# Graph attention kernel on one core: VectorE takes the next group's logits and the turned one-hots behind the fifth message instead of behind the second

## What is computed

```python
z = (x @ W).reshape(N, num_heads, head_dim)
el = jnp.sum(z * attn_l, axis=-1)
er = jnp.sum(z * attn_r, axis=-1)
e = jax.nn.leaky_relu(el[src] + er[dst], NEG_SLOPE)
m = jax.ops.segment_max(e, dst, num_segments=N)
ex = jnp.exp(e - m[dst])
denom = jax.ops.segment_sum(ex, dst, num_segments=N)
alpha = ex / denom[dst]
msg = alpha[:, :, None] * z[src]
out = jax.ops.segment_sum(msg, dst, num_segments=N)
```

## Time and profile before

| what | us |
|---|---|
| median of 3 runs (3047.36 to 3049.39) | 3047.59 |
| the profiled execution, its own time | 3049.01 |
| its span, first to last instruction | 3047.3 |
| first to last gather issue, first layer | 247.5 to 873.8 |
| the same, second layer | 1095.5 to 1721.7 |
| the same, third layer | 1937.5 to 2563.3 |

### The profile page before, as it was taken

The page is one execution under the profiler, slowest core; times in us unless marked ns, Lnnn a source line. Parts: engine busy times, 40 slices in busy tenths (PEclk is TensorE's granted clock), DMA queues, the critical chain, the costliest instruction groups (busy, mean ns, idle before and its releaser), DMA issues.

```text
span 3047.3 us, 57262 instructions
## 1 busy us (share of the span) xinstructions
PE 2681.5 (88%) x14059; PEld 1839.2 (60%) x14060; DVE 2055.3 (67%) x3890; ACT 1244.9 (41%) x2607; POOL 1495.0 (49%) x1528
## 2 busy tenths in 40 slices
PE   3997999998989979999899899788899888659998
PEld 2884555555558855555555588555555555447776
DVE  6776888888887768888878877455555555663332
ACT  1224555555554445555555544222323223521111
POOL 1005666666632156666666411466666664114443
PEclk9998999999999979999999999799999999979999
DMA  6448988989968889999989678888888998967776
GB/s 211 167 146 269 304 306 303 304 306 302 305 203 213 212 247 305 303 307 304 306 299 306 231 199 221 237 295 297 294 300 298 294 297 270 406 211 146 145 146 119
DMA packets 218702, 787.26 MB, mean 258 GB/s; under 512 B 44050, under 2 KB 75938, under 8 KB 217983
## 3 DMA queue, kind: packets, MB, share of 16 engines
q0 software_dynamic: 127632, 604.14, 63.8%
q1 hardware_dynamic: 73230, 133.39, 14.3%
q10 hardware_dynamic: 17760, 48.79, 4.0%
HBM read 665.13 MB, written 133.50 MB: 262 GB/s over the span
## 4 chain that ended last, share of the span: by engine, by line
PE 53%; DVE 22%; issue 13%; ACT 3%; another core or an unknown queue 3%; DMA 2%; SPq 2%; POOL 1%; DVEq 1%; ACTq 1%; POOLq 0%
PE PS L1026 29%; DVE arena L1466 6%; PE PS L957 5%; PE PS L1153 5%; PE PS L1142 4%; PE PS L959 3%; DVE parts L1483 3%; PE PS L1001 2%; DVE W L1466 2%; DMA arena<-table,src_k 2%; SPq L479 1%; DVE arena L1341 1%; DVE arena L1330 1%; DVE arena L1331 1%
## 5 line engine op out<-in xcount | busy, mean ns | idle before, releaser
L652 POOL DMA_INDIRECT arena<-table,src_k x945 | 946.9, 1002 | 488.6 <-issue 225.2
L1026 PE MATMUL PS<-arena,S 128*128 128x384 f32 (+1 forms) x1848 | 694.7, 509 | 58.6 <-issue 49.5
L1466 DVE TENSOR_TENSOR arena<-arena,PS 128x768 f32<-128x768 f32 x630 | 575.0, 945 | 0.9 <-issue 0.5
L1026 PEld LDWEIGHTS PS<-arena,S 128*128 128x128 f32 x1848 | 333.0, 192 | 275.3 <-issue 142.3
L1026 PE MATMUL PS<-parts,S 128*128 128x384 f32 (+2 forms) x1332 | 338.6, 374 | 54.2 <-issue 41.3
L652 POOL DMA_INDIRECT W<-table,src_k x300 | 297.8, 993 | 155.4 <-issue 68.9
L1026 PE MATMUL PS<-arena,S_weighted 128*128 128x384 f32 (+1 forms) x840 | 318.7, 515 | 35.3 <-issue 32.9
L1001 PEld LDWEIGHTS PS<-erp,ST_b 128*128 128x128 bf16 x3735 | 194.8, 97 | 240.6 <-issue 173.1
L598 POOL DMA_DIRECT2D table<-arena x75 | 41.7, 555 | 560.1 <-DVEq L1353 384.2
L809 ACT ACTIVATE apart<-iota_row,dst_k 128x128 f32<-128x128 f32 x830 | 261.5, 389 | 58.4 <-issue 34.4
L1026 PEld LDWEIGHTS PS<-parts,S 128*128 128x128 f32 x1332 | 223.5, 192 | 99.8 <-issue 90.2
(11 more groups left out here) (286 smaller groups left out, 4275.1 us busy)
## 6 DMA issues: line engine op xcount, KB each, us to landing
local_b<-local SPq DMA_DIRECT2D x249, 160.0 KB
mixed<-sums ACTq DMA_DIRECT2D x75, 384.0 KB
arena<-mixed SPq DMA_DIRECT2D x75, 384.0 KB, 4.3
table<-arena POOLq DMA_DIRECT2D x50, 396.0 KB, 3.6
arena<-table SPq DMA_DIRECT2D x50, 384.0 KB, 4.8
arena<-table,src_k POOLq DMA_INDIRECT x945
table<-arena POOLq DMA_DIRECT2D x25, 384.5 KB, 4.8
out<-last_bias POOLq DMA_DIRECT2D x25, 384.0 KB, 6.3
```

The lines of the kernel that those rows point to most:

```text
L652: nc.gpsimd.indirect_dma_start(edge_row(l, k % U)[:, 0:table_width(l)], None, table[l][:, :], bass.IndirectOffsetOnAxis(src_k[:, k:k + 1]. ...
L1026: o = nc.tensor.matmul(flat[:, bass.ds(odd * 1024 + 512 * c, n)], onehot, row[:, c * HALF:c * HALF + n], start=False, stop=True, skip_grou ...
L1466: nc.vector.tensor_tensor(z, z, a, ALU.mult).then_inc(s_msg, 1)
```

## The change

In `weigh` the calls of `turned` and of the steps leave the loop over the five messages and come behind it, the steps first and `turned` after them. Before, `turned` came behind message 1 (the second), the first step directly after it, the second step behind message 2 and, with one head, the third and fourth behind message 3.

```diff
@@ -1496,12 +1496,11 @@
                         message(g, i, jj, j)
                         if H > 1 and j >= 2 and jj * G + j - 2 in SPLIT[l]:
                             rest(g, i, jj, j - 2)
-                        if j == 1 and turn_next:
-                            turned(g + NBUF, i + 1, jj)
-                        if steps and 1 <= j <= min(3, len(steps)):
-                            steps[j - 1]()
-                        if j == 3 and steps and H == 1:
-                            steps[3]()
+                    if steps:
+                        for step in steps:
+                            step()
+                    if turn_next:
+                        turned(g + NBUF, i + 1, jj)
```

## The result

| | median, us | runs |
|---|---|---|
| before | 3048.36 | 7 (3045.02 to 3051.80) |
| changed | 3059.40 | 7 (3053.31 to 3063.23) |

The ratio is 1.003, 95% interval 1.0018 to 1.0041: the change makes the kernel slower by 0.3%. The forecast was 3045.0 us and no measurable change. The profiled execution of the changed kernel took 3053.31 us (span 3051.6), the quickest of its seven, so its trace explains 4.3 us of span, and not the other 6 or 7.

A forecast was written before the change was run, and what follows sets the result against it. Gathers in flight, about five landing every 7.5 us, were taken as the bound. Inside the sweeps 0 us, ends -0.5 - 0.5 - 1.5 = -2.5 us, from the median 3047.6 to a forecast of 3045.0 us, range 3037 to 3062.

The forecast's parts named there:

- the released messages: Inside the sweeps, three messages per group no longer held behind the gather wait; costed at nothing, slots being free 5 us early.
- the collision of `turned` with POOL: Rival: `turned` near a landing collides with POOL's gather issue, 0.7 us per group, 174 us if nothing hid it; chance 0.02.
- The price of one stall: DVE's wait for `rest` at a block's close: 2.2 us, or 3.9 us in the group of slots 10 to 14.
- 63 us a layer: DVE's stalls for `rest` at a layer's 24 closes inside the sweep, 18 x 2.2 + 6 x 3.9, 45 us more than before.
- it fits, with 42 us left: First layer: 66 us added in total against DVE's 108 us of spare time, so the sweep gets no longer.
- The chain's term: Logits, exponentials, then first message now precede every group's messages: 0.25 us more per group, 21 us over a layer's 83 groups.
- 25 to 50 us: The wait in front of the logits, line 1449, expected to remain in the changed profile.
- -0.5 us for each of the first two layers: Ends of the first two layers' edge sweeps: the middle taken between 2.8 us earlier and 1.9 us later.
- The gain of 2.8 from the held messages: End of a sweep: where DVE waits for the last landing, its end comes 2.8 us earlier.
- The third layer's -1.5: End of the third layer's sweep: a gain of 0 to 2.8 us, taken as 1.5, because PE is behind there.
- VectorE and ScalarE become the bound: Rival: stalls of `rest` behind closes in the first two layers use up DVE's spare time, 3062 to 3077 us; chance 0.28.
- All ends gain in full: Rival: each layer ends 2.8 to 4 us earlier, 8 to 12 us in all, giving 3037 to 3039 us; chance 0.25.

The follow-up runs named there:

- e2: Kernel before with only `turned` moved behind the fifth message, the steps left as before; quick gathers: 2812.49 us, ratio 0.9997 to the kernel before.
- e10: The changed kernel as it stands, run with quick gathers: 2966.93 us, ratio 1.0569 to the kernel before.
- e12: Kernel before with the new order in the last three groups of each layer alone; quick gathers: 2807.65 us, ratio 0.9996 to the kernel before.
- e15: Changed kernel with ACT's one-hots moved ahead of the exponentials; quick gathers: 2850.72 us, ratio 1.0148 to the kernel before.
- e16: Kernel before with only ACT's one-hots moved ahead of the exponentials; quick gathers: 2851.03 us, ratio 1.0158 to the unedited kernel before.
- e6: The changed kernel again, in another job with slow gathers: 3085.34 us, ratio 1.0028 to the kernel before.
- e7: Kernel before with, for 12 heads only, logits behind the fourth message, `higher` then `turned` behind the fifth; slow gathers: 3077.95 us, ratio 1.0006 to the kernel before.
- e17: Changed kernel with the second operand of the third layer's long `rest` instruction read from PSUM, timing only: 2925.79 us, ratio 1.0400 to the kernel before.
- e18: Kernel before with the second operand of the third layer's long `rest` instruction read from PSUM, timing only: 2785.02 us, ratio 0.9913 to the unedited kernel before.

## Why the prediction was wrong

**Right:** gathers set the pace inside the sweeps; the released messages buy nothing there; the collision of `turned` with POOL, which I gave 0.02, costs nothing (e2). The price of one stall was right too: I had 2.2 us beside a close and 3.9 in the group of slots 10 to 14, and e10's first layer shows 19 stalls of 2.2 to 2.4 and 4 of 3.9 to 4.0.

**The step that failed** is "63 us a layer", and with it "it fits, with 42 us left". It counted only groups with a close. In e10's first layer 16 more stalls of 1.1 us stand in groups of slots 10 to 14 without one, where `rest` comes after three messages and the one-hots alone are long enough (the row at 706.69 above). 19 x 2.3 + 4 x 4.0 + 16 x 1.1 = 77 us, the measured 76.6; in the result the stalls beside closes are some 9 us longer, to 86.0, where PE's lateness at closes comes on top. The trace of the kernel before had all the durations for it: exponentials, one-hots and `leading` follow each other in every group, not only beside a close. The chain's term, 21 us, was a little too large: 5.5 us more of waits in front of the first message, and 10.8 us more of DVE's busy time between the first and the last issue (523.8 us against 513.0), together 16.3. So 16.3 + (86.0 - 17.6) = 84.7 us were added, where 66 was forecast, and DVE's wait for the logits fell by about as much (82.5). I expected 25 to 50 us to be left; 8 were.

**The second step** is "-0.5 us for each of the first two layers". It took the state in which DVE meets the last landing from the kernel before. With nothing to spare DVE cannot catch up after a stall, and meets it 5.4 us later: +2.6 us instead of -0.5. The gain of 2.8 from the held messages was of the right size and was overrun. The third layer's -1.5 came out as -0.7.

**Rivals.** "VectorE and ScalarE become the bound" is half of what happened. Its mechanism ate all but 8 us of the spare time, but in the result the gathers still set the pace: they spread over 626 us, and its own sign was over 630. That 3059.4 us comes near its 3062 is no proof of it, since it had that time from the sweeps and the trace has it at the ends. With quick gathers (e10) it holds in full. I gave it 0.28. Its deciding point, a stall 1.75 us above 2.2 at each close, was looked for in the wrong quantity: most stalls were not longer, there were more of them. "All ends gain in full" fell. No term or rival had the third layer's `rest` beside the gather issues: the new order meets it more often, which costs 17 to 22 us with quick gathers (e10 against e12, e15 against e16), and the slow gathers of the result hid it.

**What stays open.** Of the 11 us between the medians the traces explain 4 to 5; the others of the changed kernel's executions took up to 10 us more than the one that was traced, and none of them was seen. A second pair gives a like share: e6 and e7, in one job, have spans 9.9 us apart, and the first two ends make 5.0 of it (the third, which e7 leaves as before, -3.5), the spreads 3.2 and the stretches that the change does not touch 5.2. So the loss of 0.3% is measured twice, and only some half of it is traced to the lateness at the ends. No run here tells why the same program's gathers come at 1.33 us a visit in one job and at 1.51 in another, nor what POOL waits for at 1.51; that it is a landing is my reading.

## What to carry to other kernels

When a wait for data is moved behind work, ask not only what that releases but how long the other engine's in-order list is between the thing it now gets late and the thing that is wanted back: here exponentials, one-hots, `leading`. Sum that list for every group, with and without the rare branch, against what is left of the period; an average that just fits leaves nothing to catch up with, and shows at the ends of loops first. Judge such an order, too, at the quickest pace that the transfers have been seen to keep, since a slow one covers it: 0.3% and 5.7% are the same edit. And when two kernels come out equal, compare them stretch by stretch before you call the edit neutral: e15 and e16 were equal by two differences of 20 us.

## What the hardware showed that I had not expected

The same program on this chip type runs its gathers at 1.51 to 1.54 us a visit in one job and 1.30 to 1.34 in another, and the kernel before takes 3048 to 3075 or 2807 to 2814 us with it.

A gather issue on POOL (0.95 us) takes up to 1.7 us when VectorE beside it runs an instruction with two operands in SBUF. With one of them in PSUM it does not: in e17's third layer 194 issues overlap that instruction and 82 the bf16 one-hots of line 1419, and none of them is over 1.3 us. It is not every meeting: in e10's third layer 179 issues overlap line 1487 and 62 are long. The Trainium skill, "GPSIMD Engine Reference", section "8. Key points", names two SBUF inputs as one cause of contention; e17 and e18 agree. Its other cause is a two-port mode; whether line 1419 runs in one no run here shows. No issue is long for it, but line 1419 itself is, in some places: in the result's first layer the 76 that overlap an issue take 492 ns on average and the other 7 379, while in e2's first layer all 83 overlap one and take 381. So this contention is DVE's to pay, about 0.1 us a group, and it was there before the change as well (482 ns against 376). In the kernel before the collisions of the third layer cost up to 0.9% with quick gathers (e18).
